# Dividing layer 0's attention products four tiles at a time, with the eight shares of a word laid side by side

## The reference, cut to what matters

```
kc = k.reshape(B, H, Nc, CHUNK, Dh)          # B 8, H 4, Nc 8, CHUNK 128, Dh 32
vc = v.reshape(B, H, Nc, CHUNK, Dh)
scores = clip(einsum('bhnd,bhjcd->bhnjc', q, kc) / sqrt(Dh), -10, 10)
scores = where(mask == 0, -10, scores)
attn = softmax(scores, axis=-1)              # over the 128 keys of a chunk
ctx = einsum('bhnjc,bhjcd->bhnd', attn, vc)  # sum over keys and over the 8 chunks
```

## Time and profile before

| what | value |
|---|---|
| median of 3 runs | 2969.57 us (2963.59 to 2971.39) |
| the profiled execution's own time | 2962.04 us |
| its span in the profile | 2960.2 us |
| mean granted TensorE clock | 0.847 |
| busy share: PE, PEld, DVE, ACT, POOL | 78%, 55%, 73%, 54%, 63% |
| stretch of heads(0) | about 133 to 740 us of the span |
| memory traffic | 162.84 MB read, 95.36 MB written, 87 GB/s |

### The profile page before, as it was taken

The page is one execution under the profiler, slowest core; times in us unless marked ns, Lnnn a source line. Parts: engine busy times, 40 slices in busy tenths (PEclk is TensorE's granted clock), DMA queues, the critical chain, the costliest instruction groups (busy, mean ns, idle before and its releaser), DMA issues.

```text
span 2960.2 us, 89198 instructions
## 1 busy us (share of the span) xinstructions
PE 2309.2 (78%) x32745; PEld 1617.6 (55%) x33080; DVE 2157.0 (73%) x4078; ACT 1585.4 (54%) x2273; POOL 1853.8 (63%) x1837
## 2 busy tenths in 40 slices
PE   4588888887565999999957668884659988989980
PEld 3366666666442556666635446663426665666660
DVE  4499999999464999999933354433759988888965
ACT  3344444454363555555534534444727776777775
POOL 2288888888341778777853434443318877777873
PEclk9788888888676999999976679997769998898995
DMA  7922333331575222232235421102631211111117
GB/s 245 322 69 71 77 78 78 77 77 27 127 229 172 61 63 61 63 71 64 63 77 168 136 73 52 52 16 95 156 83 50 48 45 42 46 44 42 50 31 162
DMA packets 336189, 263.48 MB, mean 89 GB/s; under 512 B 229688, under 2 KB 293432, under 8 KB 335856
## 3 DMA queue, kind: packets, MB, share of 16 engines
q1 hardware_dynamic: 331248, 241.83, 30.7%
q0 software_dynamic: 4608, 16.78, 1.5%
HBM read 162.84 MB, written 95.36 MB: 87 GB/s over the span
## 4 chain that ended last, share of the span: by engine, by line
PE 45%; issue 17%; DVE 16%; ACT 7%; SPq 5%; DMA 4%; POOL 2%; DVEq 1%; ACTq 0%; POOLq 0%
PE ps L1094 15%; PE ps L1053 7%; DVE xn L1408 4%; SPq L527 4%; PE ps L1034 3%; PE ps L1003 3%; PE ps L941 3%; ACT xn L721 2%; DVE cv L1370 2%; DVE full L1350 2%; DMA qs<-nshift 2%; PE ps L1012 2%; PE ps L1038 2%; PE ps L965 2%; PE ps L1051 2%
## 5 line engine op out<-in xcount | busy, mean ns | idle before, releaser
L329 POOL TENSOR_TENSOR xc<-part 128x512 f16<-128x512 f32 x1536 | 1604.7, 1073 | 626.6 <-ACT part L858 473.1
L1094 PE MATMUL ps<-vs,part 128*128 128x33 bf16 (+1 forms) x13824 | 845.9, 188 | 46.2 <-DVEq L1443 44.5
L1094 PEld LDWEIGHTS ps<-vs,part 128*128 128x128 bf16 x13824 | 674.0, 101 | 352.9 <-issue 207.6
L1350 DVE CUSTOM_DVE_ANT_0 full<-ps,mask_n 128x1024 bf16<-128x1024 f32 x576 | 695.5, 1218 | 150.7 <-PE ps L1003 71.8
L1094 PE MATMUL ps<-vs,xc 128*128 128x33 bf16 (+1 forms) x9216 | 775.5, 186 | 9.5 <-issue 9.5
L1094 PEld LDWEIGHTS ps<-vs,xc 128*128 128x128 f16 x9216 | 593.9, 99 | 6.8 <-issue 6.8
L840 ACT ACTIVATE part<-cv,lift 128x1024 f32<-128x1024 f32 x256 | 294.8, 1152 | 321.5 <-DVE cv L1370 298.5
L858 ACT ACTIVATE part<-ps 128x512 f32<-128x512 f32 x512 | 305.6, 597 | 281.3 <-PE ps L1038 281.3
L1053 PE MATMUL ps<-qs,sel 128*128 128x512 f32 x640 | 416.0, 651 | 17.0 <-ACT ps L832 17.0
L1034 PE MATMUL ps<-qs,ks 128*128 128x512 f32 x512 | 287.9, 565 | 123.3 <-DVE cv L1370 91.4
L1382 DVE SCALAR_TENSOR_TENSOR cv<-ks,colx,ps 128x512 f32<-128x512 f32 x320 | 238.7, 746 | 182.9 <-PE ps L1053 145.9
(11 more groups left out here) (145 smaller groups left out, 3313.7 us busy)
## 6 DMA issues: line engine op xcount, KB each, us to landing
qs<-q_d SPq DMA_DIRECT2D x224, 128.0 KB
ks<-k_d SPq DMA_DIRECT2D x224, 128.0 KB
ks<-row_d SPq DMA_DIRECT2D x40, 512.0 KB
vs<-v_d SPq DMA_DIRECT2D x96, 198.0 KB
q_d<-part SPq DMA_DIRECT2D x32, 512.0 KB
k_d<-part SPq DMA_DIRECT2D x32, 512.0 KB
ctx_d<-xn SPq DMA_DIRECT2D x96, 128.0 KB, 1.8
xc<-ctx_d SPq DMA_DIRECT2D x96, 128.0 KB, 4.4
```

Of the source, the lines that this page charges most:

```text
L329: eng.tensor_tensor(plo[:, r, :], prob[:, r, :], phi[:, r, :], ALU.subtract).then_inc(low_done(layer, u, s)[0], 1)
L1094: mm = pe.matmul(acc, half[:, r, it * P:(it + 1) * P], vs[:, n, at:at + width], start=opens and h == 0 and v == 0, stop=h == 1 and v == 1, ...
L1350: dve.tensor_tensor_reduce(junks[k % 2], src, mask_n[:, k, :], 1.0, least, ALU.add, ALU.max, accum_out=dst).then_inc(s_nmax, 1)
```

## The change

Four tiles are divided at once. In PSUM each tile's 132 result columns now start at a half bank (256 columns), so tiles s mod 8 fill banks 4 to 7 and four tiles are two banks. `weigh` waits every fourth tile, for the group of four that is two groups before; `blocks_done` is called for every fourth tile and does 16 reciprocals and one product of 512 words. `rden` grows from 8 to 16 words. `blk` becomes [partition, t, d, j] with j innermost: the product writes each element 8 words (32 bytes) after the one before, and the sum reads 1024 words in a row. HCHAIN and HLEFT of layer 0 follow the smaller number of links (36 to 20, 7 to 4). Nothing else is changed.

```diff
-HCHAIN = (36, 32, 52, 28)
-HLEFT = (7, 4, 6, 3)
+HCHAIN = (20, 32, 52, 28)
+HLEFT = (4, 4, 6, 3)
...
-        blk = work[:, :, :].rearrange("p j (t d) -> p j t d", d=32)
+        blk = work[:, :, :].rearrange("p j n -> p (j n)").rearrange("p (t d j) -> p t d j", d=32, j=BLOCKS)
...
-                            if j % 2 == 0:
-                                pe.wait_ge(s_chfree, CREDIT + u * (TILES // 2 * UNROLL) + s // 2 - 3)
+                            if j % 4 == 0:
+                                pe.wait_ge(s_chfree, CREDIT + u * (TILES // 4 * UNROLL) + s // 4 - 1)
...
-                                acc = ps[:, 4 + s // 2 % 4, (s % 2 * IB + it) * 33:(s % 2 * IB + it + 1) * 33]
+                                at = 4 * HALF + s % 8 * 256 + it * 33
+                                acc = pf[:, at:at + 33]
...
-                        acc = ps[:, 4 + s // 2 % 4, 0:2 * IB * 33].rearrange("p (a d) -> p a d", d=33)
+                        acc = pf[:, (4 + s // 4 % 2 * 2) * HALF:][:, 0:2 * HALF].rearrange("p (j w) -> p j w", j=4)[
+                            :, :, 0:IB * 33].rearrange("p j (t d) -> p j t d", d=33)
+                        r = rden[:, :].rearrange("p (j t) -> p j t", j=4)
                         dve.wait_ge(s_av, tile_value(s) + 1)
-                        dve.wait_ge(s_chfree, CREDIT + u * (TILES // 2 * UNROLL) + s // 2)
-                        link(dve.reciprocal(rden[:, 0:2 * IB], acc[:, :, 32]))
-                        dve.tensor_tensor(blk[:, j - 1:j + 1, :, :],
-                                          acc[:, :, 0:32].rearrange("p (j t) d -> p j t d", j=2),
-                                          rden[:, 0:2 * IB].rearrange("p (j t) -> p j t", j=2).unsqueeze(3
-                                          ).to_broadcast([P, 2, IB, 32]), ALU.mult).then_inc(s_chfree, 1)
+                        dve.wait_ge(s_chfree, CREDIT + u * (TILES // 4 * UNROLL) + s // 4)
+                        link(dve.reciprocal(r, acc[:, :, :, 32]))
+                        dve.tensor_tensor(blk[:, :, :, j - 3:j + 1].rearrange("p t d j -> p j t d"),
+                                          acc[:, :, :, 0:32], r.unsqueeze(3).to_broadcast([P, 4, IB, 32]), ALU.mult
+                                          ).then_inc(s_chfree, 1)
...
                             ins = dve.tensor_reduce(
                                 outp[:, n % 2, c * IB * 32:(c + 1) * IB * 32].rearrange("p (t d) -> p t d", d=32),
-                                blk[:, :, :, :].rearrange("p j t d -> p t d j"), AX.X, ALU.add)
+                                blk[:, :, :, :], AX.X, ALU.add)
...
-                            if layer == 0 and e % 2:
+                            if layer == 0 and e % 4 == 3:
                                 blocks_done(e)
```

More of the change, by code:

```diff
@@ L191, in build @@
         nshift = sb("nshift", [P, 2, BLOCKS])
-        rden = sb("rden", [P, 8])
-        blk = work[:, :, :].rearrange("p j (t d) -> p j t d", d=32)
+        rden = sb("rden", [P, 16])
+        blk = work[:, :, :].rearrange("p j n -> p (j n)").rearrange("p (t d j) -> p t d j", d=32, j=BLOCKS)
         sums = work[:, 0:3, :].rearrange("p v f -> p (v f)").rearrange("p (t v d) -> p t v d", t=IB, v=3)
@@ L1393, in blocks_done @@
                         c, j = tt // BLOCKS, tt % BLOCKS
-                        acc = ps[:, 4 + s // 2 % 4, 0:2 * IB * 33].rearrange("p (a d) -> p a d", d=33)
+                        acc = pf[:, (4 + s // 4 % 2 * 2) * HALF:][:, 0:2 * HALF].rearrange("p (j w) -> p j w", j=4)[
+                            :, :, 0:IB * 33].rearrange("p j (t d) -> p j t d", d=33)
+                        r = rden[:, :].rearrange("p (j t) -> p j t", j=4)
                         dve.wait_ge(s_av, tile_value(s) + 1)
-                        dve.wait_ge(s_chfree, CREDIT + u * (TILES // 2 * UNROLL) + s // 2)
-                        link(dve.reciprocal(rden[:, 0:2 * IB], acc[:, :, 32]))
-                        dve.tensor_tensor(blk[:, j - 1:j + 1, :, :],
-                                          acc[:, :, 0:32].rearrange("p (j t) d -> p j t d", j=2),
-                                          rden[:, 0:2 * IB].rearrange("p (j t) -> p j t", j=2).unsqueeze(3
-                                          ).to_broadcast([P, 2, IB, 32]), ALU.mult).then_inc(s_chfree, 1)
+                        dve.wait_ge(s_chfree, CREDIT + u * (TILES // 4 * UNROLL) + s // 4)
[3 more added lines that the diff above has]
+                                          ).then_inc(s_chfree, 1)
                         if j == BLOCKS - 1:
-                            dve.wait_ge(s_chfree, CREDIT + u * (TILES // 2 * UNROLL) + s // 2 + 1)
+                            dve.wait_ge(s_chfree, CREDIT + u * (TILES // 4 * UNROLL) + s // 4 + 1)
                             U = UNIT0[layer] + u * UNROLL + n
```

## The result

The changed kernel takes 3024.93 us (median of 4, 3018.82 to 3029.34) against 2970.48 for the kernel before: ratio 1.017, 95% interval 1.0116 to 1.0224. It is 54 us slower, where 33 us less was forecast, and lies above the range. The profiled executions stand at 3024.92 and 2962.04 us, 62.9 apart.

What follows compares the result with a forecast made beforehand. VectorE, 93% busy in layer 0's heads, was taken as the bound. Eight tiles: 9.09 - 8.48 - 0.10 for a new wait = 0.51 us less, 64 times, 33 us; forecast median 2937 us, range 2908 to 2988.

Steps and rivals of the forecast that it cites:

- Other layers don't use `blk`, and their links are counted as before.: Stages outside layer 0's heads: claimed untouched by the change, so no time was forecast for them.
- The strided write: VectorE's product in layer 0's heads, writing every word 8 words past the last: its cost per word decides the sign.
- The middle case: Product writes cost like the strided read, 1.78 ns a word: 0.98 us each, 33 us faster in all; chance 0.34.
- The dear case: Rival: product writes cost twice the strided read's excess, 2.53 ns a word: 17 us slower, 2987; chance 0.30.
- The fills of the earlier trace: Evidence for a free strided write: a 32-word fill with a 198-byte step takes 85 ns, like fills in a row.
- The sum: VectorE's sum of 1024 words, read in a row: near 1215 ns instead of 1989, 1.36 us instead of 2.13.
- The reciprocals: VectorE's reciprocals, four of 8 words becoming two of 16: 0.24 us each, 0.48 instead of 0.92 per eight tiles.
- The new wait: TensorE's `weigh` waits for the group's division, delaying VectorE at the low clock: 0.10 us per eight tiles.
- ScalarE and GpSimd live on tiles already settled: Layer 0's heads: claimed both engines stay fed despite TensorE's added wait; no time was charged for them.
- The 0.21 left ... lies where one loop body follows another: Layer 0's heads: 9.28 us measured against 9.07; the rest, about 13 us in all, lies between loop bodies.
- The forecast's own range: Total of 2922 to 2950 us, from an added wait between 0 and 0.25 and a write at 1.7 to 1.9.
- "same": Outcome not told from no change, about 0.3% or 9 us: chance 0.02 plus 0.12.

Runs made afterwards that it cites:

- after_pad: Changed kernel with 82 already met waits in TensorE's stream between heads(0) and node(1): 2969.38 us, ratio 1.0001 to the kernel before.
- before_pad: Kernel before with 430 already met waits in TensorE's stream between heads(0) and node(1): 3028.01 us, ratio 1.0198.
- swap: Changed kernel, padded with met waits, each group's division issued on VectorE ahead of the settle of its turn instead of behind it: 2960.24 us, ratio 0.9971.
- late: Kernel before with both divisions of four tiles issued together behind every second settle, size and place untouched: 3010.46 us, ratio 1.0183.
- pairs_runs: Kernel before, division in pairs, with the new layout and key block innermost in the product, writing two adjacent words: 2926.73 us, ratio 0.9864.
- runs: Changed kernel, padded with met waits, product reordered to write runs of four adjacent words: 2960.24 us, ratio 0.9971 to the kernel before.
- runs_r: As runs, with the 16 reciprocals also stored key block innermost: 2916.50 us, ratio 0.9844 to the kernel before.

## Why the prediction was wrong

- *"Other layers don't use `blk`, and their links are counted as before."* This step failed and gave the sign. It took an untouched stage for an unmoved one. TensorE's loop for layer 1 moved by 41 instructions and was read again on each of its five returns, which cost 61 us (after_pad and before_pad); that it then lay in an eighth packet is how the stops in the trace are read. No rival spoke of it. The 4.29 MB of the instruction queue stood on the page of before, and heads(0), whose TensorE loop of 2811 instructions is 11 packets long, took 97 of the 262 packets there: the sign of loops that don't stay was to be seen.
- *The strided write.* The middle case was right: 1129 ns long against 1.07 us, 0.96 from start to start against 0.98. The dear case fell. The fills of the earlier trace rows misled a little in the other direction. At 0.86 ns a word, 32 words would have cost 28 ns more than a fill in a row, and the fill shows nothing of it; why not is open. Two of the three fills are bf16, and none reads anything.
- *The sum*, from the comparison of a read from SBUF with one from PSUM: 1220 ns and 1.34 us, right.
- *The reciprocals*: 0.28 us, forecast 0.24.
- *The new wait*: its mechanism was there (20.2 us for TensorE), its price of 0.10 a round (6 us) lies within what swap allows (2 to 9 us).
- *"ScalarE and GpSimd live on tiles already settled"* and, behind it, TensorE's 6.7 us for eight tiles held against a round of 8.5: this was the second failed step, and it took the forecast gain of 33 us (after_pad gained nothing). Averages over a round were compared where the store between TensorE and VectorE is four tiles deep. Two settles in a row outrun TensorE by 1.67 - 1.14 = 0.53 us at the full clock, and in the time of the sum TensorE can lay up four tiles and no more. Measured: 9.02 us a round in after_pad without what lies between bodies, against 8.58, which is also the sum of VectorE's measured steps (4.56 + 0.56 + 0.96 + 1.16 + 1.34), so 0.44 is waiting. late shows by itself that bunching costs; why a store of four tiles can't carry it over is argued, not tried.
- *"The 0.21 left ... lies where one loop body follows another"*: right. Part of the reason is likely TensorE's branch back, which stands 3.3 to 3.9 us on each of the five returns in heads(0) of the kernel before, against 0.22 in heads(1).
- The forecast's own range, 2922 to 2950, comes out of its terms as 2925 to 2955. Nothing hangs on it.
- The chances: 0.60 on faster was wrong by both steps. Without the moved loop the result would have been "same", 0.14.

## What to carry to other kernels

A change that removes instructions moves every loop behind it on that engine: where a stage that wasn't touched gets slower, look at "issue" waits, at how long the loop's branch takes and at the packets of the instruction queue, and move the loop with met waits before anything is concluded on the change itself. With a shallow store between two engines, don't bunch work that was spread evenly: divided behind every second settle instead of every settle, the kernel before lost 1.8%, somewhat over a quarter of it to VectorE's own extra work and the rest to waiting. When a layout turns a strided read into a strided write, reorder the loop of the writer so that it writes at least two adjacent words, and give the small operand the same order.

## What the runs showed of the hardware

- TensorE's loop of 1584 instructions (6.19 packets of 16384 bytes) ran without being read again from two starts, with a branch back of 0.22 us, and was read again on each of its five returns from two others, with a branch back of 5.05 us and a second stop of 1.6 to 2.9: 552 against 613 us for the stage. The two slow starts are 256 instructions apart. With the packets' edges as the second stop shows them, the loop stays when it touches seven packets and doesn't at eight. The loop of 2811 instructions (11 packets) in heads(0) was read again in both kernels, with branches back of 3.3 to 4.2 us.
- VectorE writing single f32 words to SBUF in steps of 32 bytes costs 0.86 ns a word in duration ((1129 - 691) / 512), runs of two or more cost nothing (427 and 691 ns). The Trainium skill (Vector Engine (DVE) Microarchitecture Reference, Measured stream behaviour on trn2) says the same of runs of two; its 2.50 ns a word for small steps of 24 words was not met at steps of 8 words: 1.03 + 0.86 = 1.89.
- Reading single words of SBUF in turn from two places costs nothing (427 ns in pairs_runs), from four places 0.77 ns a word ((1084 - 691) / 512, runs against runs_r), from eight 0.75 (the sum of before). Reading PSUM with a hop at every word costs nothing in any of them.
